# Three grouped attentions of a transformer: another order of their first score tiles, fills and kept maxima, and long score tiles paired with short ones

## The reference

```python
x = x + window_attention(layernorm(x))      # L0_attn
x = x + swiglu(layernorm(x))                # L0_ffn
x = x + causal_attention(layernorm(x))      # L1_attn
x = x + spline_experts(layernorm(x))        # L1_ffn
x = x + causal_rope_attention(layernorm(x)) # L2_attn
x = x + latent_experts(layernorm(x))        # L2_ffn
x = x + scrambled_attention(layernorm(x))   # L3_attn, not causal, with a bias
x = x + routed_experts(layernorm(x))        # L3_ffn

# each of the three grouped attentions, 16 heads of 16 channels:
scores = einsum('bhqd,bhkd->bhqk', q, k) / sqrt(16)
p = softmax(mask(scores))                   # mask only where it is causal
x = x + einsum('bhqk,bhkd->bhqd', p, v) @ Wo
```

## Time and profile before

| what | value |
|---|---|
| median of three runs | 1846.48 us (1842.49 to 1853.06) |
| the profiled execution | 1844.27 us, span 1842.5 us |
| PE busy | 1619.7 us, 88% of the span |
| DVE busy | 1141.2 us, 62% |
| ACT busy | 867.1 us, 47% |
| POOL busy | 469.0 us, 25% |
| mean granted clock of TensorE | 0.946 of full speed |

### The profile page before, as it was taken

How to read it: one execution, slowest core, us unless ns; L and a number is a source line. 1 busy time by engine, 2 the same in 40 slices (tenths; PEclk the granted TensorE clock), 3 DMA queues, 4 the chain that set the end, 5 groups by cost and what they waited for, 6 DMA issues and landing times. The chain is left out here.

```text
span 1842.5 us, 28977 instructions
## 1 busy us (share of the span) xinstructions
PE 1619.7 (88%) x10726; PEld 957.3 (52%) x10726; DVE 1141.2 (62%) x2567; ACT 867.1 (47%) x1358; POOL 469.0 (25%) x596
## 2 busy tenths in 40 slices
PE   4899999799989999843999999779999999998776
PEld 2344444488856666542455665457764444443533
DVE  2787877333456566377577765465545688774475
ACT  1356665433325555450255455357751666665322
POOL 4222210033322330011333220047762422300000
PEclk9999999999989999965999999789999999999798
DMA  7452350200335523001543450302206335320222
GB/s 245 107 127 71 83 134 1 95 0 0 103 81 144 155 79 90 1 9 43 160 134 91 111 148 2 104 26 71 86 1 186 91 83 148 114 47 19 105 93 92
DMA packets 68962, 160.30 MB, mean 87 GB/s; under 512 B 10286, under 2 KB 15927, under 8 KB 67963
## 3 DMA queue, kind: packets, MB, share of 16 engines
q1 hardware_dynamic: 68826, 158.51, 30.3%
HBM read 109.05 MB, written 53.09 MB: 88 GB/s over the span
## 5 line engine op out<-in xcount | busy, mean ns | idle before, releaser
L1155 DVE TENSOR_REDUCE a_mx<-PS 128x1 f32<-128x512 f32 (+3 forms) x768 | 395.0, 553 | 190.0 <-PE PS L1411 123.4
L1348 ACT ACTIVATE a_pT<-PS 128x1024 f32<-128x1024 f32 (+3 forms) x384 | 310.5, 811 | 215.1 <-PE PS L1435 153.1
L1406 PE MATMUL PS<-a_k,a_q 64*128 64x512 f32 (+3 forms) x768 | 234.5, 418 | 17.3 <-DVE a_mx L1155 13.4
L440 DVE CUSTOM_DVE_ANT_0 PS<-PS,a_dist 128x448 f32<-128x448 f32 x256 | 156.2, 643 | 50.9 <-PE PS L685 48.5
L1426 PE MATMUL PS<-a_q,a_k 64*128 64x512 f32 (+3 forms) x768 | 173.1, 437 | 9.3 <-issue 5.0
L1449 PE MATMUL PS<-a_pT,a_va 128*32 128x512 f32 (+3 forms) x1536 | 164.2, 499 | 5.6 <-ACT a_raw L1305 5.4
L590 ACT ACTIVATE a_pT<-PS 128x448 f32<-128x448 f32 (+1 forms) x256 | 124.7, 540 | 84.6 <-PE PS L708 84.2
L1406 PEld LDWEIGHTS PS<-a_k,a_q 64*128 64x128 f32 x768 | 111.5, 187 | 80.6 <-DVE a_mx L1155 62.5
L1426 PEld LDWEIGHTS PS<-a_q,a_k 64*128 64x128 f32 x768 | 75.1, 184 | 146.1 <-issue 71.1
L157 PE MATMUL PS<-cst 128*128 128x512 f32 x192 | 106.2, 686 | 36.6 <-PEq L98 28.6
L2335 POOL TENSOR_TENSOR f_h_low<-f_prod,f_h_high 128x512 fp32r<-128x512 f32 x84 | 110.2, 1318 | 59.6 <-ACT f_h_high L2522 57.1
(11 more groups left out here) (361 smaller groups left out, 3455.9 us busy)
## 6 DMA issues: line engine op xcount, KB each, us to landing
spread_scratch<-a_high SPq DMA_DIRECT2D x96, 256.0 KB, 2.9
a_q<-spread_scratch SPq DMA_DIRECT2D x96, 256.0 KB, 5.4
a_k<-spread_scratch SPq DMA_DIRECT2D x96, 256.0 KB, 6.4
f_gb<-gate_rows SPq DMA_DIRECT2D x68, 256.0 KB, 4.8
spread_scratch<-a_low SPq DMA_DIRECT2D x48, 256.0 KB, 3.7
a_q<-window_scratch SPq DMA_DIRECT2D x32, 256.0 KB, 5.6
a_k<-window_scratch SPq DMA_DIRECT2D x32, 256.0 KB, 6.4
window_scratch<-a_high SPq DMA_DIRECT2D x24, 256.0 KB, 4.7
```

Of the source, the lines that this page charges most:

```text
L440: dve.tensor_tensor_reduce(PS[:, 4 + a, 0:KW], PS[:, 4 + a, 0:KW], dt_[:, off:off + KW], 1.0, 3e38, ALU.add, ALU.min, mx[:, gg % 2, qt, 2 ...
L1155: dve.tensor_reduce(mx[:, gg % 2, qt, 2 * half + a:2 * half + a + 1], PS[:, 4 + a, 0:kw], AX.X, ALU.max).then_inc(max_done, 1)
L1348: act.activation(pT[:, N // 2 % 2, N % 2, :, q0:S], PS[:, 2 * (N % 2):2 * (N % 2) + 2, q0:S], ACT.Exp, scale=SCALE).then_inc(exp_done, 1)
L1406: mm = pe.matmul(ps[:, 0:kw], q[b % 2][rows, pair, qt * P:(qt + 1) * P], k[b % 2][rows, pair, 0:kw], start=True, stop=not causal)
```

## The change

Five edits, all of them in the three grouped attentions and in the swiglu stage that hosts the front of a1.

1. `tile_of` gives the causal attentions another order of tiles: a tile of 512 stands beside one of 128, and one of 384 beside one of 256, in place of two equal ones. Which row group has the long tile alternates from pair to pair.
2. `tile_bank`: the first 24 tiles of an attention use banks 4, 5 and 2 in turn, so that tile t waits for the reduction of tile t-3 and no longer of t-2. `scores_T(1)`, the first to use bank 2, waits for the last of these reductions.
3. `fill_rest`: the two fills of POOL leave `loop` and stand, in a2 and a3, behind the other fills early in the front. In a1 they stay where they are.
4. `keep_maxima(0, 0)` on DVE stands ahead of the reductions of the last four of the 24 tiles, and no longer behind them; in the swiglu stage `turn_maxima(0, 0)` on PE moves ahead of the scores of these four tiles.
5. `ready`: ACT runs an exponential of one column ahead of `keep_maxima(0, 0)`.

```diff
         def tile_of(t):
 
             j = t % (2 * TB * 2)
+            if causal:
+                far = (j // 2 % 2) ^ (j % 2)
+                long = TB - 1 - j // 8
+                return t // (4 * TB), TB - 1 - long if far else long, j // 4 % 2, j % 2
             return t // (4 * TB), TB - 1 - j // 4, j // 2 % 2, j % 2
+
+        def tile_bank(t):
+
+            return (4, 5, 2)[t % 3] if t < LEAD else 4 + t % 2
...
-            def loop():
+            def fill_rest():
                 pool.memset(zeros[:, :], 0.0).then_inc(preset, 1)
                 pool.memset(va[1][:, :, :, :], 1.0).then_inc(preset, 1)
                 pool.wait_ge(preset, 6)
+
+            def loop():
...
-                dve.tensor_reduce(mx[:, gg % 2, qt, 2 * half + a:2 * half + a + 1], PS[:, 4 + a, 0:kw], AX.X,
+                dve.tensor_reduce(mx[:, gg % 2, qt, 2 * half + a:2 * half + a + 1], PS[:, tile_bank(t), 0:kw], AX.X,
...
+            def ready():
+
+                act.activation(ln.held[:, 1:2], neg_half[:, 0:1], ACT.Exp)
...
-                if t >= 2:
-                    pe.wait_ge(max_done, t - 1)
-                ps = PS[:, 4 + a, :]
+                if t >= (2 if t >= LEAD else 3):
+                    pe.wait_ge(max_done, t - 1 if t >= LEAD else t - 2)
+                ps = PS[:, tile_bank(t), :]
...
+                if N == 1:
+                    pe.wait_ge(max_done, LEAD)
...
                 def _(pool):
                     p = pool_program(pool)
-                    if not hosted:
+                    if hosted:
+                        p.fill_rest()
+                    else:
                         p.norm()
                         p.fill()
+                        p.fill_rest()
                         p.turned_units()
...
-                        for t in range(4 * TB, LEAD):
+                        for t in range(4 * TB, 4 * TB + 4):
                             p.maxima(t)
                         p.keep_maxima(0, 0)
+                        for t in range(4 * TB + 4, LEAD):
+                            p.maxima(t)
...
                         p.keep_values(0, 1, value_banks[1])
+                        p.ready()
                         p.keep_maxima(0, 0)
...
-                    for s in range(max(0, 8 * t - 4), min(24, 8 * t + 4)):
+                    for s in range(max(0, 8 * t - 4), min(20, 8 * t + 4)):
                         following.maxima(s)
                 following.keep_maxima(0, 0)
+                for s in range(20, 24):
+                    following.maxima(s)
...
                 hidden_high(NB - 1, NHT - 1)
+                following.ready()
                 following.keep_maxima(0, 0)
...
                         if t and n % 4 == 3:
+                            if t == TB - 1 and n == NHT - 1:
+                                following.turn_maxima(0, 0)
                             for s in range(8 * t + n - 11, 8 * t + n - 7):
                                 following.scores(s)
-                following.turn_maxima(0, 0)
```

More of the change, by code:

```diff
@@ L1136, in loop @@
                         layer_norm_pool(pool, ln, N // STEPS + 2, neg_half)
-            p.norm, p.fill, p.turned_units, p.norm_next, p.split_maxima, p.loop = (
-                norm, fill, turned_units, norm_next, split_maxima, loop)
+            p.norm, p.fill, p.fill_rest, p.turned_units, p.norm_next, p.split_maxima, p.loop = (
+                norm, fill, fill_rest, turned_units, norm_next, split_maxima, loop)
             return p
@@ L1359, in scalar_program @@
             p.weights_high, p.input_high, p.keep_unit, p.keep_masks = weights_high, input_high, keep_unit, keep_masks
-            p.keep_values, p.keep_maxima, p.loop = keep_values, keep_maxima, loop
+            p.keep_values, p.ready, p.keep_maxima, p.loop = keep_values, ready, keep_maxima, loop
             return p
```

## The result

The changed kernel takes 1831.96 us in the median of 16 runs (1824.88 to 1841.34), the kernel before 1845.85 us in its 16 (1839.69 to 1860.28). The ratio is 0.9917, with a 95% interval of 0.9900 to 0.9935: 13.9 us faster by the medians, where 17.8 were forecast from the profiled execution. The profiled execution of the changed kernel took 1827.52 us with a span of 1825.7, that is 16.8 less than the one before.

What follows compares the result with a forecast made beforehand. PE's instruction list bounds the loops of a1 and a2. Fronts -1.5 (a1), -3.3 (a2), -6.8 (a3), table in a3 -0.2 and loops -6 sum to -17.8, from 1844.27 to 1826 us; range 1815 to 1841, likeliest case 1818 to 1834.

Steps and rivals of the forecast that it cites:

- a2's front: Front of a2: moved fills end the stall and keep the clock up, -3.3 us, bounds 0 and -0.7.
- a3's front: Front of a3: stall -2.1, unblocked pairs -1.5, full clock for fillers, transposes and score pairs; sum -6.8 us.
- the table: First exponentials of a1 and a3: early exponential hides the 1.28 us table load, -0.3 and -0.2 us.
- roughly cancel: a2's front: the last tile's new wait for DVE's earlier 1.23 us copy, against fillers having hidden that copy before: net about nothing.
- the bound of -0.7: a2's front: -3.3 + 2.6 us, if the new wait brings the clock down again.
- the signs that it named for being right: Fronts: normalization 0.41 us, no stalls, full clock, a3's pairs 1.49 apart, no table load; a1, a2 loops some 3 us less.
- a1's front: Swiglu tail's six fours: third bank and narrower partners shorten waits, -1.2 us; with the table, -1.5.
- The loops: Loops of a1 and a2, 7.6 batches: shorter bank waits outweigh unequal pairs, about -6 us, bounds +8 and -13.
- B: a3's front: sixteen bias additions hold the fourth normalization for 10.96 us in the fills' place; 1839 us, chance 0.18.
- C: Causal loops: unequal pairs cost their longer tile and the waits stay, +8 us; 1840 us, chance 0.13.
- D: Score pairs: unequal tiles don't run beside each other, +60 us over 30 groups; 1892 us, chance 0.06.
- E: Fronts of a2 and a3: something other than the fills holds the normalization, stalls stay; about 1835 us, chance 0.07.

Runs made afterwards that it cites:

- The fills alone: Only POOL's two fills moved into the fronts of a2 and a3, against the kernel before: ratio 0.9964, 7.2 us by the medians.
- the pairs alone: Only the new order of score tiles in the causal attentions, against the kernel before: ratio 0.9980.
- kept maxima late again: The changed kernel with DVE's kept maxima behind the last four reductions again and the turn behind the swiglu tail's last scores: ratio 0.9892 to the kernel before.
- the third bank alone: Only the third bank for the first 24 tiles, with its waits, against the kernel before: ratio 0.9974.
- the additions in their place: The kernel before with a3's sixteen bias additions ahead of the two fills in POOL's loop: one run, 1837.61 us.
- the one that was made to tell them apart: Old tile order in groups 1 and 2 of a1's first batch, in the changed kernel with one filler before the fronts' last tile, none behind: ratio 0.9864 to the kernel before.

## Why the prediction was right, and where its terms were off

**The sign, the range and the main mechanism** were right: the fills, not the additions, held batch 1's normalization, and behind it PE and its clock. The fills alone gave 3.7 and 5.8 us in the fronts of a2 and a3 (3.4 in a3 against the profile of the pairs alone, with its shorter half clock). That the sum fits so well, 17.8 against 16.8 in the profiles and 13.9 in the medians, is in part luck: a2's front and a1's loop each fell short by more than 1 us, and the half clock in a3 that the forecast counted back was longer than in two other profiles with the same stall. The page "SBUF — State Buffer" of the Trainium skill, section "Who interferes with whom", says that a two-port DVE operation and a GpSimd operation exclude each other for a whole instruction. The holding for a whole instruction agrees with the trace: a fill did it (2.52 and 0.77 us, each to just behind the fill's end), and so did the POOL operation of 1.30 us (a subtraction) that had begun 0.14 us ahead of the first normalization of the earlier trace rows. An addition that began behind the normalization was itself the one to wait. That the first issuer wins doesn't show in the recorded starts: by these the fills began behind the normalization that they held. Whether the normalization ran in such a two-port mode no row shows.

**a3's front**, -6.8 and -0.2 for the table, came out at -7.3. The pairs gave 1.55 us as forecast, and the stall went. The clock's share, some 3 us of the sum, was counted from the one profile with 10.1 us at half; against the profile of the pairs alone the front gains 5.0. The table gave nothing there.

**a2's front**, -3.3, came out at -2.0. The step that failed is the sentence that the copy's move and the fillers "roughly cancel". They don't: PE waits 1.27 us for the copy, and the fillers, which hid it before, now only stand ahead of `scores_T`. At the full clock this costs 0.8 us (a3, kept maxima late again), and in a2 the clock fell in the wait, 1.5 more; the bound of -0.7 for that case had been put down, and the truth lay between. The unequal pairs cost 0.8 in this front, which the sum had at nothing. That it still came to -2.0 is owed to the fills, which alone gave 3.7, and, by what is left, to the third bank. At 1.99 us earlier, a2's first `scores_T` lies, by a hundredth, under the 2 us below which the prediction called itself wrong. Of the signs that it named for being right, the clock at full speed in a2's front and some 3 us less in a1's loop did not come.

**a1's front**, -1.5, came out at -1.4, but by two errors: the third bank alone gives 2.45, and the unequal pairs take 1.1 of it back, since the last tile of a four waits for the reduction of the first, which is now a 512 or a 384 in every four.

**The loops**, -6, came out at -4.5. Step by step, from the starts of `scores_T` in both traces outside the first batch of a1, the terms are as forecast: the step behind a kept maximum -0.135, the step with the second long pair -0.40, an unequal pair about +0.06 where 256 became 384 and +0.03 to 0.14 where 128 did. Two were missed: +0.22 in place of 0.11 in the fourth step of a batch, and, in a1, -0.08 in the two other long steps of a group together (in a2 -0.53 to +0.03). In all the second batch gained 0.87 in a1 and 1.27 in a2, where 0.6 and 0.85 were forecast.

**What was mis-sized** is a1: -0.5 where these steps would have given over 2. There the clock ran at half speed for 13.8 us from the loop's start, where it had been 8.6 before, and the forecast had said that the clock stays as it was. With equal pairs in the first steps it was 3.6, and the loop took 4.1 us less than with unequal ones there.

**The rivals.** B fell with the fills alone and with the additions in their place. C fell with a2's loop in the pairs alone; in a1 they gave 2.1 us in the later batches, and the first batch took it back. D fell with the pair at 618.97: two unequal tiles take 0.51 together. E fell with the normalization at 0.41.

## What to carry to other kernels

Look for one long instruction among equal ones (2515 ns among three of 406): what ran beside it on another engine is the thing to move, and behind such a stall the half clock can cost as much as the stall. When an instruction is moved ahead so that a waiting engine gets it earlier, look at what hid it before: fillers that covered a wait are pure delay once the wait has moved ahead of them, and moving one and leaving out the rest gave 7.3 us in the two fronts, against 9.3 that the whole change gave there. Compare stretches step by step, and look at the granted clock of each before a gain is put down to an edit: here the same front differed by 2.4 us between two profiles by the clock alone, and a gain that showed in one of two like loops was missing from the other in its first steps.

## What the runs showed of the hardware that was not expected

- A fill on POOL holds a normalization on DVE to 0.15 us behind the fill's end, though by the trace the normalization had started 0.11 us earlier; with an addition that starts 0.13 us behind it, the addition is the one that is held, by 0.14. Whether the kind of instruction or these 20 ns decide was not told apart.
- Where PE sat idle for 1.09 to 1.39 us ahead of the last of the 24 tiles in the fronts of a2 and a3, TensorE's clock fell to 1.2 GHz behind it in three of six fronts (the changed kernel and those without the pairs and without the early exponential); with an idle time of 0.22 to 0.55 in their place it fell in none of eight.
- In the six profiles with unequal pairs in the first steps of a1's loop, TensorE's clock was back at 2.4 GHz 13.8 to 17.0 us behind its start; in the six without, 8.0 to 11.0, and in the one that was made to tell them apart 3.6. That equal pairs go with the earlier rise is shown by all thirteen, each profiled once; by what they do it is not shown.
